# The last three of a tile's four result transfers wait for the matching chunks of the tile two places on

## The reference, cut to what matters

```python
logits = flat @ router_w.T                      # 8 experts
topk_probs, topk_idx = jax.lax.top_k(softmax(logits), 2)
h1 = einsum('nc,ehc->neh', flat, w1); h3 = einsum('nc,ehc->neh', flat, w3)
h = silu(h1) * h3                               # 682 hidden channels
y = einsum('neh,ech->nec', h, w2)
out = einsum('ne,nec->nc', gates, y)            # the two chosen experts, weighted
```

## Time and profile before

| | |
|---|---|
| median of 3 runs | 988.93 us (986.78 to 991.55) |
| the profiled execution | 986.66 us |
| its span, first to last instruction | 984.9 us |
| mean granted TensorE clock | 0.929 |
| TensorE busy | 847.8 us (86%) |
| VectorE busy | 603.6 us (61%) |
| ScalarE busy | 476.8 us (48%) |
| GpSimd busy | 412.0 us (42%) |

### The profile page before, as it was taken

How to read it: one execution, slowest core, us unless ns; L and a number is a source line. 1 busy time by engine, 2 the same in 40 slices (tenths; PEclk the granted TensorE clock), 3 DMA queues, 4 the chain that set the end, 5 groups by cost and what they waited for, 6 DMA issues and landing times.

```text
span 984.9 us, 24041 instructions
## 1 busy us (share of the span) xinstructions
PE 847.8 (86%) x8576; PEld 518.0 (53%) x8576; DVE 603.6 (61%) x1386; ACT 476.8 (48%) x933; POOL 412.0 (42%) x524
## 2 busy tenths in 40 slices
PE   4774799999999689969989778789999999999940
PEld 4444587777778556648777633223333333333530
DVE  1352587877878456745797855568565565655634
ACT  1042476666666434534554345445555555555520
POOL 0000345455454211100355556656666754444470
PEclk9885799999999789999989979989999999999985
DMA  7226200000000398000000030212031221111108
GB/s 192 57 63 121 51 9 11 10 9 11 8 11 3 119 339 255 2 3 2 16 18 21 22 74 23 58 41 54 25 76 44 57 50 38 45 38 45 42 3 256
DMA packets 103437, 57.22 MB, mean 58 GB/s; under 512 B 68261, under 2 KB 97793, under 8 KB 103360
## 3 DMA queue, kind: packets, MB, share of 16 engines
q1 hardware_dynamic: 89920, 46.61, 18.1%
q0 software_dynamic: 9088, 8.55, 2.7%
q10 hardware_dynamic: 4352, 1.05, 0.5%
HBM read 26.02 MB, written 28.97 MB: 56 GB/s over the span
## 4 chain that ended last, share of the span: by engine, by line
PE 33%; DMA 6%; POOL 5%; issue 4%; DVE 4%; ACT 2%; SPq 0%; ACTq 0%; POOLq 0%; DVEq 0%
PE bank L1350 18%; PE bank L1360 9%; DMA slot_x<-rows,slots 5%; POOL slot_x L1226 3%; PE bank L1336 2%; POOL chosen_out L1234 2%; PE bank L1369 2%; DVE norm_T L1755 1%; DMA ex_x<-slot_x 1%; PE bank L1283 1%; ACT norm_T L1465 1%; DVE residual L1772 1%; PE bank L1256 1%; DVE norm_T L1770 1%; DMA norm_T<-chosen_out 0%
## 5 line engine op out<-in xcount | busy, mean ns | idle before, releaser
L1755 DVE TENSOR_TENSOR norm_T<-norm_T,bank 114x512 f32<-114x512 f32 (+7 forms) x234 | 143.1, 636 | 150.7 <-ACT norm_T L1465 147.2
L1350 PE MATMUL bank<-ex_xt,ex_w 64*114 64x512 f32 (+7 forms) x936 | 214.9, 583 | 17.0 <-DVE norm_T L1755 13.5
L1234 POOL DMA_INDIRECT chosen_out<-ex_out,ex_id x156 | 155.8, 999 | 135.2 <-DVE ex_out L1707 74.3
L1465 ACT ACTIVATE norm_T<-bank 114x512 f32<-114x512 f32 (+7 forms) x234 | 129.7, 558 | 82.6 <-PE bank L1350 81.8
L1226 POOL DMA_INDIRECT slot_x<-rows,slots x128 | 123.8, 968 | 108.8 <-issue 63.8
L1350 PEld LDWEIGHTS bank<-ex_xt,ex_w 64*114 64x114 f32 x936 | 76.7, 177 | 106.4 <-issue 86.2
L462 POOL TENSOR_TENSOR probs<-shifted,win_rden 128x512 f32<-128x512 f32 x64 | 66.7, 1043 | 104.1 <-DVE win_rden L656 97.5
L1360 PE MATMUL bank<-norm_T,ex_w 114*64 114x512 f32 (+7 forms) x468 | 102.7, 574 | 0.3 <-ACT ex_w L1452 0.3
L1360 PEld LDWEIGHTS bank<-norm_T,ex_w 114*64 114x64 f32 x468 | 30.4, 139 | 69.2 <-issue 52.0
L642 DVE TENSOR_REDUCE win_max<-ps_s 128x8 f32<-128x512 f32 x64 | 43.9, 686 | 36.5 <-PE ps_s L502 36.5
L1458 ACT ACTIVATE norm_T<-bank 128x512 f32<-128x512 f32 (+7 forms) x39 | 21.8, 559 | 80.7 <-PE bank L1360 80.7
(11 more groups left out here) (261 smaller groups left out, 1499.2 us busy)
## 6 DMA issues: line engine op xcount, KB each, us to landing
slot_x<-blank SPq DMA_DIRECT2D x1, 17028.0 KB, 56.4
ex_x<-slot_x SPq DMA_DIRECT2D x39, 132.0 KB, 2.7
ex_x<-slot_x SPq DMA_DIRECT2D x39, 128.0 KB, 2.7
norm_T<-chosen_out SPq DMA_DIRECT2D x8, 512.0 KB, 6.8
w_in<-in_L_ffn_w_dram SPq DMA_DIRECT2D x24, 168.0 KB
chosen_out<-ex_out,ex_id POOLq DMA_INDIRECT x156, 2.2
wlocal_in<-in_L_conv_w_local_dram SPq DMA_DIRECT2D x2, 1152.0 KB, 7.3
norm_T<-in_x_dram SPq DMA_DIRECT2D x4, 512.0 KB, 8.9
```

What stands on the lines that cost most here:

```text
L1234: eng.indirect_dma_start(s.chosen_out[:, :], bass.IndirectOffsetOnAxis(ex_id[k % OUTS][:, j:j + 1].bitcast(U32), 0), out[k % OUTS][:, j, : ...
L1350: eng.matmul(ps[b][0:HCHUNK, 0:width(k)], w13[par][halves(i), c * HCHUNK:(c + 1) * HCHUNK], xt[par][halves(i), 0:width(k)], start=True, st ...
L1465: eng.activation(act[c % DEEP][:, 0:width(k)], ps_1[c % DEEP][0:HCHUNK, 0:width(k)], ACT.Silu).then_inc(act_n, 1)
L1755: eng.tensor_tensor(h[par][:, c, 0:width(k)], act[c % DEEP][:, 0:width(k)], ps_3[c % deep3(k)][0:HCHUNK, 0:width(k)], ALU.mult).then_inc(h ...
```

## The change

Ahead of the second, third and fourth transfer of `scatter(k)` stands a wait on `h_n`. Transfer j of tile k waits until chunk j of tile k+2 has gone through VectorE's multiplication, for j = 1, 2 and 3. The first transfer is as it was. The scatters of the last two tiles, 37 and 38, have no tile two places on and are as they were. So 37 x 3 = 111 waits are added, all on GpSimd's queue; nothing is taken out and nothing is moved.

```diff
                 def scatter(k):
                     eng.wait_ge(oc_n, k + 1)
                     for j in range(R):
+                        if j > 0 and k + 2 < FTILES:
+                            eng.wait_ge(h_n, HCHUNKS * (k + 2) + j + 1)
                         eng.indirect_dma_start(s.chosen_out[:, :], ...)
```

## The result

The changed kernel took 993.4 us in the median of 20 runs (988.52 to 1001.81), the kernel before 988.15 us (984.74 to 992.1, 20 runs). The ratio is 1.0056, with a 95% interval of 1.0034 to 1.0078. The profiled execution took 992.18 us, its span is 990.4 us, 5.5 us longer than before. That is the forecast side, inside the range, at half of the forecast size: 5.3 us between the medians where 10.5 stood in the sum.

What follows compares the result with a forecast made beforehand. GpSimd's in-order queue was taken to bound the first tiles, TensorE the stretch from 668 to 935 us, GpSimd the tail. 4.54 + 4.35 + 1.6 = 10.5 us made 997.2 profiled, 999 us by the median; range 992 to 1006.

Steps and rivals of the forecast that it cites:

- (a): `scatter(0)`: fourth transfer held for chunk 3 of tile 2, 4.94 us later; `scatter(1)` then starts 4.54 us later.
- (b): `scatter(1)`: its waits cost nothing, but part 4 lands late; TensorE's idle before tile 5 grows by 4.54 us.
- (c): `scatter(2)`: fourth transfer held for chunk 3 of tile 4, 9.69 us late; `scatter(3)` starts 7.19 us late.
- (d): `scatter(3)`: fourth transfer held for chunk 3 of tile 5, going 9.37 us late.
- (e): `scatter(4)` to `scatter(11)`: no wait binds, GpSimd stays 9.37 us late; TensorE stands 4.2 to 4.5 us at tile 13.
- (g): Steady state: fourth transfer goes 2.1 us later, hidden in GpSimd's idle time of 4.59 us per tile.
- (h): Tail from 935.80: GpSimd is the bound, but the chunks waited for are done in time; 0 us.
- The 0.13 us beside the sum: `scatter(0)`'s fourth transfer leaves VectorE's weight copy, which would lower the sum by 0.13 us; not counted.
- the second term: TensorE's new stop before tile 13, because part 6 is complete 9.37 us later: +4.35 us.
- (f): Granted clock falls behind the new stop at tile 13: +1.6 us, from 0 to 4.4; nothing new at tile 5.
- The forecast case (two stalls): TensorE's stops before tiles 5 and 13 both cost time, with a clock fall: 10.5 us; chance 0.70.
- the rival with one stall: Only tile 5's stall comes, none at tile 13: 4.5 us more, 991.2 or by the median 993.5; chance 0.11.

Runs made afterwards that it cites:

- two_three: Changed kernel with the three waits only in `scatter(2)` and `scatter(3)`; ratio 1.0016 to the kernel before, 989.53 us.
- fourth_only: Changed kernel with only the fourth transfer waiting, the second and third not; ratio 1.0056 to the kernel before.
- from_twelve: Changed kernel with waits only in `scatter(12)` and later, 75 of the 111; ratio 1.0012 to the kernel before, median 988.03 us.
- order_b: Kernel before with the sends of parts 4 to 7 moved ahead and all 111 waits added; ratio 0.9939, 980.55 us.
- first_only: Changed kernel with the three waits in `scatter(0)` alone; ratio 1.0039 to the kernel before, 991.38 us.
- again: Changed kernel unaltered, run and profiled a second time; ratio 1.0064 to the kernel before, 994.93 us.
- two_later: Changed kernel with transfer j waiting for chunk j+2 instead of chunk j; ratio 1.0198 to the kernel before, 1009.35 us.

## Why the prediction was half right

**Right.** In the changed kernel's profile the mechanism held at each place where it was forecast: (a) `scatter(0)` held by chunk 3 of tile 2, (b) `scatter(1)` not held, TensorE's stop at tile 5 at 8.54 us against 8.84, (c) and (d) `scatter(2)` and `scatter(3)` held (in both profiles of the changed kernel; in two_three and fourth_only (d) did not come), (e) no fourth transfer held in the tiles behind, a new stop at tile 13, (g) and (h) nothing in the steady part and the tail. The start-up behind an unfulfilled wait was 0.78 us, not 0.86. That fulfilled waits are free is shown by the 0.30 us in `scatter(1)`, by from_twelve and by order_b. The 0.13 us beside the sum came as the row had it: `scatter(0)`'s fourth transfer took 0.98 us, away from the copy. All 156 result transfers together took 155.8 us before and 155.7 after.

**Wrong: the second term, +4.35 us, in step (e).** The mis-sized quantity is tile 13's slack, which I read as 0.3 to 0.6 us. It can be read from several executions. All times are from their timelines: TensorE's restart at tile 5, the issue of the second load of tile 13, and TensorE's turn-in of tile 13 with the stop before it.

```
kernel        restart   load of 13   between   late   without   turn-in   stop
before        630.65    715.77       85.1      3.1    82.0      719.15    0
from_twelve   628.74    711.12       82.4      0.9    81.5      717.68    0
first_only    634.93    717.33       82.4      0.7    81.7      723.85    0
two_three     631.57    716.68       85.1      1.0    84.2      720.37    0
fourth_only   634.41    719.29       84.9      0.8    84.1      722.16    0.40
changed       633.93    721.84       87.9      1.8    86.1      724.77    2.03
again         639.37    726.03       86.7      1.3    85.4      729.02    2.27
two_later     642.56    735.68       93.1      1.0    92.2      738.46    6.88
```

"Late" is by how much GpSimd's waits for the landing of a piece of `send`, between restart and load, were longer than 2.0 us, added up; "without" is "between" less that.

Without waits at `scatter(2)` and `scatter(3)` GpSimd needs 82.4 us, in two executions. TensorE needs some 88.9 us (717.68 - 628.74; 723.85 - 634.93), and the load takes 2.9 us to land (721.84 to 724.77 in the changed kernel). The room is 88.9 - 82.4 - 2.9 = 3.6 us. The one profile of before had 85.1 us and 0.5 us of room. The reason stands in its GpSimd timeline, in two landings that were longer than the usual 2.0 us of idle time:

```profile
672.34 1.23 POOL L1234 DMA_INDIRECT chosen_out<-ex_out,ex_id  x1 [3.74 <-DMA slot_x<-rows,slots]
...
715.07 0.99 POOL L1234 DMA_INDIRECT chosen_out<-ex_out,ex_id  x1 [3.28 <-DMA slot_x<-rows,slots]
```

1.7 + 1.3 = 3.0 us were chance of that execution; the others have 0.7 to 1.8 us. I took them for fixed and added the whole delay on top. GpSimd came to tile 13's load 87.9 - 82.4 = 5.5 us later in the changed kernel than in first_only. 3.6 of it fill the room, and 5.5 - 3.6 = 1.9 us is the stop of 2.03 us.

The 5.5 us are not all the waits' doing. With late landings taken off it is 86.1 - 81.7 = 4.4 us, and 85.4 - 81.7 = 3.7 in again, against 9.37 - 4.54 = 4.8 forecast. The other 1.1 us are late landings, this time against the changed kernel. With none at all, in either, the room would be 88.9 - 81.7 - 2.9 = 4.3 us, and the waits would just fill it (an estimate from the table's rows). So the waits bring tile 13 to the edge, and how long TensorE stands there is decided by what else differs between executions: the landings, whether `scatter(3)` is held, and TensorE's own time, which was only 87.4 us in again and fourth_only. The stop was 0.40, 2.03 and 2.27 us in the three profiles with every fourth transfer's wait.

**Wrong in part: (f).** The 1.6 us of clock were due in one profile of two. The granted clock stayed at 1.00 behind an idle time of 2.03 us; behind one of 2.27 us it fell (0.63 and 0.52 in the windows from 730 to 734 of again), and the products took the times of the lower level. The Trainium skill, TensorE: Matmul & The Clock Gate, in its part on why the gate matters for a kernel, warns of idle gaps between bursts of products that bring the half rate back, and it names gaps longer than both of these. The stops before tile 5 agree with it (0.50 behind 4.30 and behind 8.54 us). The fall behind 2.27 us goes beyond it, and there the measurement decides. At tile 5 the slow clock cost 0.45 + 1.57 = 2.02 us in the changed kernel against 0.39 + 1.24 = 1.63 before, where (f) put nothing; two_three has 2.13 us behind a stop of only 4.77, so the length of the stop isn't what makes the difference.

With the room put right the sum would be 4.5 + 1.9 + half of 1.6 = 7.2 us. The medians have 5.3, with 3.4 to 7.7 by the interval. The remaining 1.9 us lie within it. The forecast case (two stalls) was the right one by its mechanism; in size the result lies nearest to the rival with one stall (4.5 us), which is not what the profiles show. That 993.4 us lies inside the range is owed in part to this rival: the range was drawn down to 992 to take it in, and not because the sum allowed for a short second stop.

The rivals: fulfilled waits are free; the waits do reach TensorE; there are two stalls in the changed kernel, the second a short one.

## What to carry to other kernels

A wait on an in-order queue costs what stands behind it and is needed soon; price it there, and look for the first place where a consumer is already waiting. Where it only uses up slack, take the slack from several executions or from the typical landing, since one profile can hold three microseconds of chance (3.1 us before, 0.7 in first_only). And a queue that carries both the inputs of later tiles and the results of earlier ones is to send the inputs first: that alone gave 0.5% here (0.9946 and 0.9954).

## What was not expected of the hardware

A transfer of GpSimd that waits for VectorE's count starts 0.78 us after the counted instruction ends, where back-to-back transfers are 0.30 us apart. A piece of six or four indirect transfers was usually landed and seen 2.0 us after the last one's end, but in the profile of the changed kernel two such idle times were 2.74 and 3.03 us, and in that of before 3.28 and 3.74. Ahead of the longest, Sync had issued a tile's two loads at 665.29 and 666.29, just before the piece's last transfer at 667.64. The same holds for the 3.03 us (loads at 689.66 and 690.30, last transfer at 690.72), but not for the 3.28 us, whose last transfer at 710.83 had no load near it. Whether that is the cause wasn't tried.

The granted clock can fall behind an idle time of 2.27 us. It can also stay or fall behind the same short ones: behind 1.06 and 0.61 us, with four products between, four products took 1.12 us in the changed kernel (at 660.14) and 1.58 in first_only (at 659.66), where the next window, 660 to 662, has a clock of 0.55.
